# A macaron block on one core: V of the first half, the second half's tiles and the later tokens' transposes in the first half's slots

## What is computed

```python
x = x + 0.5 * ffn(layernorm(x))          # dense 512x512 + top-2 of 8 LoRA experts of rank 16
q = rope((n @ wq).reshape(B, S, 32, 128)); k = rope((n @ wk).reshape(B, S, 8, 128))   # n = layernorm(x)
v = (n @ wv).reshape(B, S, 8, 128)
scores = q . k * 128 ** -0.5, masked to j <= i and j > i - 128
x = x + (softmax(scores) @ v).reshape(B, S, 4096) @ wo
x = x + 0.5 * ffn(layernorm(x))
```

## Time and profile before

| | us |
|---|---|
| median of 3 runs (lowest, highest) | 746.47 (746.28, 747.5) |
| the profiled execution | 746.33 |
| its span in the trace | 744.6 |

### The profile page before, as it was taken

One profiled execution on the slowest core, in us unless ns is written; L12 is line 12 of the kernel. 1 busy time (PEld: TensorE's weight loads), 2 busy tenths in 40 slices (PEclk: granted clock), 3 DMA queues, 4 the chain that ended last, 5 costly groups with the idle time before them and its releaser, 6 DMA issues.

```text
span 744.6 us, 13949 instructions
## 1 busy us (share of the span) xinstructions
PE 717.2 (96%) x3692; PEld 603.1 (81%) x3692; DVE 601.0 (81%) x2060; ACT 413.3 (56%) x1122; POOL 396.5 (53%) x466
## 2 busy tenths in 40 slices
PE   8899789999999999999999999999999999998998
PEld 5787667888888888888888888888888888887786
DVE  6898778877887888878887888788878887788795
ACT  3324475657655676556655766576656665754320
POOL 0674268634864477438653765367535863462420
PEclk9999999999999999999999999999999999999999
DMA  8240003100220022002200120013000310030002
GB/s 266 73 158 16 0 3 98 43 1 2 73 70 1 0 70 70 0 0 70 56 14 0 56 70 14 0 32 94 15 0 0 99 28 1 1 114 1 0 31 85
DMA packets 25843, 32.13 MB, mean 43 GB/s; under 512 B 5833, under 2 KB 14281, under 8 KB 25298
## 3 DMA queue, kind: packets, MB, share of 16 engines
q1 hardware_dynamic: 25232, 30.69, 13.1%
q10 hardware_dynamic: 578, 1.05, 0.4%
HBM read 27.54 MB, written 4.19 MB: 43 GB/s over the span
## 4 chain that ended last, share of the span: by engine, by line
PE 70%; DVE 20%; issue 5%; ACT 3%; DMA 1%; POOL 1%; DVEq 0%; SPq 0%; ACTq 0%
PE bank L1102 26%; PE bank L1160 19%; PE bank L1145 6%; PE bank L1124 5%; PE bank L1068 5%; PE bank L1132 3%; DVE prob L822 2%; DVE rot L787 2%; DVE oT_lo L834 2%; DVE prob L814 1%; DVE sm L807 1%; PE bank L1121 1%; DVE rot L778 1%; ACT prob L550 1%; DVE pT_hi_lo L828 1%
## 5 line engine op out<-in xcount | busy, mean ns | idle before, releaser
L368 POOL TENSOR_TENSOR swap<-swap,rope 128x512 f32<-128x512 f32 x80 | 110.1, 1377 | 129.8 <-ACT swap L523 129.8
L550 ACT ACTIVATE prob<-sm,nmax 128x128 f32<-128x128 f32 x128 | 51.5, 403 | 151.4 <-DVE prob L814 150.4
L375 POOL TENSOR_SCALAR_AFFINE_SELECT pT_hi_lo<-pT_hi_lo 128x256 fp32r<-128x256 f32 x128 | 52.3, 409 | 140.3 <-DVE pT_hi_lo L828 139.8
L523 ACT ACTIVATE swap<-bank 64x512 f32<-64x512 f32 x160 | 94.9, 593 | 10.6 <-PE bank L1102 6.7
L558 ACT ACTIVATE pT_hi_lo<-bank 128x256 fp32r<-128x256 f32 x128 | 48.9, 382 | 71.5 <-PE bank L1132 50.6
L822 DVE TENSOR_SCALAR prob<-prob,rinv 128x128 f32<-128x128 f32 x256 | 83.3, 367 | 4.5
L385 POOL TENSOR_TENSOR q_lo<-rot,q_hi 128x512 fp32r<-128x512 f32 x64 | 82.6, 1291 | 6.9 <-ACT q_hi L531 6.9
L1160 PE MATMUL bank<-wo_hi,oT_hi 128*128 128x512 f32 x256 | 74.6, 413 | 5.0 <-DVE x L841 5.0
L828 DVE TENSOR_TENSOR pT_hi_lo<-bank,pT_hi_lo 128x256 fp32r<-128x256 f32 x128 | 53.6, 418 | 29.4 <-ACT pT_hi_lo L558 29.2
L1102 PE MATMUL bank<-xnT_hi,wq_hi 128*128 128x512 f32 x256 | 71.4, 391 | 2.2 <-DVE v_lo L798 1.4
L1102 PE MATMUL bank<-xnT_lo,wq_hi 128*128 128x512 f32 x256 | 73.4, 389 | 0.0
(11 more groups left out here) (150 smaller groups left out, 1768.9 us busy)
## 6 DMA issues: line engine op xcount, KB each, us to landing
raw<-in_L_attn_wq SPq DMA_DIRECT2D x32, 256.0 KB, 3.0
raw<-in_L_attn_wo SPq DMA_DIRECT2D x32, 256.0 KB, 2.6
x<-in_L_attn_x SPq DMA_DIRECT2D x4, 512.0 KB, 7.3
raw<-in_L_attn_wk SPq DMA_DIRECT2D x8, 256.0 KB, 2.7
raw<-in_L_attn_wv SPq DMA_DIRECT2D x8, 256.0 KB, 2.6
out<-x SPq DMA_DIRECT2D x8, 256.0 KB, 2.0
raw<-in_L_ffn_W_base ACTq DMA_DIRECT2D x4, 256.0 KB, 5.1
wb_keep_hi<-q_hi SPq DMA_DIRECT2D x1, 1024.0 KB, 4.9
```

The costliest lines, as they stand in the source:

```text
L368: nc.gpsimd.tensor_tensor(w, w, tab, ALU.mult).then_inc(t2_done, 1)
L523: last = nc.scalar.activation(swap[a:a + half, m % 2, :], A[m % 2][b:b + half, :], ACT.Copy)
L550: last = nc.scalar.activation(prob[:, s % 2, lo:hi], src, ACT.Exp, bias=nmax[:, s % 2, i:i + 1], scale=-1.0, accum_out=rsum[:, s % 2, i:i ...
```

## The change

The prologue projects only k and q of the first half (60 matmuls) and goes on to `scores(0)`. V of the first half (12 matmuls) and the transposes of tokens 6 and 7 go into slot 0 of group 0, and the six tiles of the second half follow in slots 1 to 7 in chunks of 12, 12, 12, 12, 12, 8 and 4 (`START`), not 9 in each of eight slots. `v_transpose(0)` and `v_hi`, `v_lo` go from slot 0 to slot 1, `v_transpose(0)` ahead of that slot's projection. The rstd of tokens 4 to 7 goes from VectorE to POOL, behind `rope_lo(0,0)`. The normalised tokens 6 and 7 are written in four half-width instructions into other places (one new tile, `spare`), and the transposes of tokens 4 to 7 go to banks 4 to 7. The SyncE queue is unchanged.

```diff
+START = (60, 72, 84, 96, 108, 120, 132, 140, 144)
+START_ENDS = {s: t for t in range(5, 12) for s in range(SLOTS) if START[s] < 12 * (t + 1) <= START[s + 1]}
...
+        spare = sb("spare", [P, 2 * P])
...
-            if ln == 1 and 4 <= t < 6:
-                return S[t % 2]
-            if ln == 1 and t >= 6 or ln == 2 and t >= 2:
+            if ln == 1 and t >= 4:
+                return bank[t]
+            if ln == 2 and t >= 2:
                 return bank[4 + t % 2]
...
+        def xn_half(ln, t, a):
+            if ln == 1 and t == 6:
+                return (sm, prob)[a][:, 1, 0:2 * P]
+            if ln == 1 and t == 7:
+                return ar_part[:, :, :].rearrange("p a n -> p (a n)")[:, 0:2 * P] if a else spare[:, :]
+            return xn_buf(ln, t)[:, a, :]
...
+        def tile_ends(g, hf, s, first, last):
+            if last and hf == 1:
+                return (0, None, 0), (0, None, 0)
+            if first and hf == 0:
+                split, end = START_ENDS.get(s - 1) if s > 1 else None, START_ENDS.get(s)
+                return tuple((t // 6, t % 6, t // 6) if t is not None else (0, None, 0) for t in (split, end))
+            return tuple((2 * g + hf + 1, ENDS.get(c), 1 - hf) for c in (s - 1, s))
... POOL, prologue
-            for m in range(6):
-                if m < 5:
-                    rope_sin(0, m)
-                if m:
-                    rope_lo(0, m - 1, 0)
+            pool.wait_ge(tables_landed, 32)
+            rope_sin(0, 0)
+            rope_sin(0, 1)
+            rope_lo(0, 0, 0)
+            norm_rstd(1, 4, NT)
+            rope_lo(0, 1, 0)
+            rope_sin(0, 2)
+            rope_sin(0, 3)
+            rope_lo(0, 2, 0)
+            rope_sin(0, 4)
+            rope_lo(0, 3, 0)
+            rope_lo(0, 4, 0)
... ScalarE, slots
+                        if start and s == 1:
+                            v_hi(0, 0)
                         softmax_exp(u, s)
-                        if s == 0:
+                        if start and s == 0:
+                            rope_hi(0, 2, 0)
+                            rope_swap(0, 4)
+                            x_hi(1, 6)
+                            x_hi(1, 7)
+                            rope_hi(0, 3, 0)
+                        elif s == 0:
                             v_hi(2 * g + hf, hf)
...
                         if m == 5:
-                            v_copy(2 * g + hf + 1)
+                            v_copy(jm)
+                            if start and s == 0:
+                                rope_hi(0, 4, 0)
... ScalarE, prologue: now swap(0,0), swap(0,1), hi(0,0), swap(0,2), hi(0,1), swap(0,3), x_hi(1,4), x_hi(1,5)
... VectorE, slots
-                        if s == 0 and not (last and hf == 1):
+                        if s == (1 if first and hf == 0 else 0) and not (last and hf == 1):
                             v_lo(2 * g + hf, hf)
...
                         softmax_norm(u, s)
                         if split is not None and split < 5:
-                            rope_sum(2 * g + hf + 1, split)
+                            rope_sum(js, split)
+                        if start and s == 0:
+                            rope_sum(0, 3)
+                            rope_cos(0, 4)
+                            x_lo(1, 6)
+                            x_lo(1, 7)
+                            rope_sum(0, 4)
... VectorE, prologue
             rope_cos(0, 0)
             norm_stats(1, NT - 2)
+            norm_stats(1, NT - 1)
             rope_sum(0, 0)
             rope_cos(0, 1)
-            norm_stats(1, NT - 1)
             rope_sum(0, 1)
             rope_cos(0, 2)
-            norm_rstd(1, 4, NT)
+            dve.wait_ge(rstd_done, 4)
             xn(1, 4)
             xn(1, 5)
+            rope_cos(0, 3)
+            softmax_min(0, 0)
             rope_sum(0, 2)
-            rope_cos(0, 3)
             xn(1, 6)
             xn(1, 7)
             x_lo(1, 4)
             x_lo(1, 5)
-            rope_sum(0, 3)
-            rope_cos(0, 4)
-            x_lo(1, 6)
-            x_lo(1, 7)
-            rope_sum(0, 4)
-            v_diff(0)
-            softmax_min(0, 0)
... TensorE, slots
-                        if s == 0 and not start:
+                        if s == (1 if first and hf == 0 else 0):
                             v_transpose(j)
-                        if start and s == 0:
-                            pe.wait_ge(xlo_done, 2 * NT)
-                        if not (last and hf == 1):
+                        if first and hf == 0:
+                            if s == 1:
+                                pe.wait_ge(xlo_done, 2 * NT)
+                            jp = START[s] // 72
+                            project(jp, jp, START[s] - 72 * jp, START[s + 1] - 72 * jp, 0)
+                            if s == 0:
+                                x_transpose(1, 6)
+                                x_transpose(1, 7)
+                        elif not (last and hf == 1):
                             project(j + 1, 1 - hf, FIRST[s], FIRST[s + 1], g + hf)
...
-                        if s == 0 and start:
-                            v_transpose(j)
... TensorE, prologue
             x_transpose(1, 4)
             x_transpose(1, 5)
-            project(0, 0, 60, 60 + 8, 0)
-            pe.wait_ge(x_out, 6)
-            x_transpose(1, 6)
-            x_transpose(1, 7)
-            project(0, 0, 60 + 8, 72, 0)
             scores(0, 0, 0, 0)
```

More of the change, by code:

```diff
@@ L401, in group @@
                     for s in range(SLOTS):
-                        split, m = (ENDS.get(c) if not (last and hf == 1) else None for c in (s - 1, s))
+                        (js, split, par), (jm, m, _) = tile_ends(g, hf, s, first, last)
                         if m is not None and m < 5:
-                            rope_sin(2 * g + hf + 1, m)
+                            rope_sin(jm, m)
                         if last and hf == 1 and s in (1, 5):
@@ L409, in group @@
                         if split is not None and split < 5:
-                            rope_lo(2 * g + hf + 1, split, 1 - hf)
+                            rope_lo(js, split, par)
                         weights(g, hf, s, last)
@@ L572, in group @@
                         start = first and hf == 0
+                        if start and s == 1:
+                            v_hi(0, 0)
                         softmax_exp(u, s)
-                        if s == 0:
+                        if start and s == 0:
[5 more added lines that the diff above has]
+                        elif s == 0:
                             v_hi(2 * g + hf, hf)
                         weights(g, hf, s, last, (0, 1))
-                        split, m = (ENDS.get(c) if not (last and hf == 1) else None for c in (s - 1, s))
+                        (js, split, par), (jm, m, _) = tile_ends(g, hf, s, first, last)
                         if m == 5:
-                            v_copy(2 * g + hf + 1)
+                            v_copy(jm)
+                            if start and s == 0:
+                                rope_hi(0, 4, 0)
                         elif m is not None:
-                            rope_swap(2 * g + hf + 1, m)
+                            rope_swap(jm, m)
                         if not (start and s == 0):
@@ L624, in _ @@
             act.wait_ge(kept, 32)
[L625 to L637, removed]
+            rope_swap(0, 0)
+            rope_swap(0, 1)
+            rope_hi(0, 0, 0)
+            rope_swap(0, 2)
+            rope_hi(0, 1, 0)
+            rope_swap(0, 3)
+            x_hi(1, 4)
+            x_hi(1, 5)
             group(0, True, False)
@@ L688, in xn @@
                 i = NT * ln + t
-                wait(dve, tr_done, i - 1)
-                nc.vector.tensor_scalar(xn_buf(ln, t), x[:, t, :].rearrange("p (a n) -> p a n", a=2), mv[:, t, 0:1], rstd[:, t:t + 1],
-                                        ALU.subtract, ALU.mult).then_inc(xn_done, 1)
+                if ln != 1 or t < 6:
+                    wait(dve, tr_done, i - 1)
+                if ln == 1 and t >= 6:
+                    for a in range(2):
+                        last = nc.vector.tensor_scalar(xn_half(ln, t, a), x[:, t, a * 2 * P:(a + 1) * 2 * P], mv[:, t, 0:1],
+                                                       rstd[:, t:t + 1], ALU.subtract, ALU.mult)
+                    last.then_inc(xn_done, 1)
+                else:
+                    nc.vector.tensor_scalar(xn_buf(ln, t), x[:, t, :].rearrange("p (a n) -> p a n", a=2), mv[:, t, 0:1],
+                                            rstd[:, t:t + 1], ALU.subtract, ALU.mult).then_inc(xn_done, 1)
             def x_lo(ln, t):
@@ L863, in group @@
                         start = first and b == 0
-                        split, m = (ENDS.get(c) if not (last and hf == 1) else None for c in (s - 1, s))
-                        if s == 0 and not (last and hf == 1):
+                        (js, split, _), (jm, m, _) = tile_ends(g, hf, s, first, last)
```

(3 more changed lines are left out.)

8 lines of the change are left out of this document (4 added, 4 removed).

## The result

The changed kernel takes 750.44 us (median of 5; 750.12 to 752.66), the kernel before 747.3 in the same comparison (746.28 to 747.61, 5 executions). The ratio is 1.0049, 95% interval [1.0033, 1.0065]: slower, by 0.5%. The profiled execution is the 750.44 one, its span 748.7 us, 4.1 more than before.

The account below looks back on a forecast made before the run. It took the loop VectorE, ScalarE, VectorE to bound the first eight slots and TensorE the rest from 123.4 us; 1.6 + 1.5 + 1.2 = +4.3 us on 746.33 gave 750.6, taken as 750.5, range 745.2 to 752.2.

Parts of the forecast that it names:

- One event decides: From 123.4 us on TensorE is the bound; moving the start of `v_transpose(1)`, 123.44 us, moves the end by as much.
- The removal from VectorE gains nothing: Prologue: with the rstd on POOL, `xn(1,4)` still ends at about 76.2 us, as before; `xn(1,5)` ends over 1 us later.
- Term one: Prologue to slot 1: `softmax_min(2)` starts at 96.2 instead of 94.66 us, +1.6 us; at full clock -0.1.
- the sign of being right: New profile: a TensorE stall of 3 to 4 us, ended by the subtraction of `v_diff`, with half clock behind it.
- half clock: TensorE at 1.2 instead of 2.4 GHz behind the stall at `v_transpose(0)`: 1.7 us lost in the 12 matmuls of k.
- Terms two and three: Slot 4 waits for the added swap and cos, +1.5 us; port waits on wo_lo in slots 5 and 6, +1.2 us.
- T: The start of `softmax_norm(4)`, at 105.73 us in the kernel before; times in slots 4 to 6 count from it.
- The sum: At `v_transpose(1)`: 1.6 + 1.5 + 1.2 = +4.3 us, giving 750.6, taken as 750.5 us.
- two cases of one kernel: Behind the stall at `v_transpose(0)`: half clock, 750.5 us, chance 42 in 100; or clock stays up, 749.0 us, 27.
- The faster rival: Prologue: VectorE, freed of 4.7 us of rstd, starts the loop 2.3 us earlier; about 744.3 us, chance 13 in 100.

Follow-up runs that it names:

- e9: The changed kernel with the rstd of tokens 4 to 7 back on VectorE and nothing in its place on POOL: 751.59 us, ratio 1.0065.
- e1: The changed kernel with 11 matmuls of no use put ahead of `v_transpose(0)`, into TensorE's stall in slot 1: 749.57 us, ratio 1.0041.
- e2: The changed kernel with `START` set so that the six second-half tiles end in the same slots as before the change: 748.22 us, ratio 1.0019.
- e5: The changed kernel with the edits of e2, e3 and e4 together: 745.02 us, ratio 0.9982.
- e10: e5 with matmuls of no use in two stalls, rstd on VectorE, and POOL's `rope_lo(0,1)` held until both `xn` are done: 743.58 us, ratio 0.9966.
- e3: The changed kernel with `v_transpose(0)` behind slot 1's 12 matmuls and `v_hi(0)` behind that slot's exponentials: 749.48 us, ratio 1.0040.
- e4: The changed kernel with POOL's `rope_lo(0,1)` waiting until the normalisation of tokens 4 and 5 is done: 750.64 us, ratio 1.0043.
- e8: The changed kernel with POOL's four wo_lo of slot 4 in group 0 waiting until `softmax_norm(5)` is done: 750.23 us, ratio 1.0043.

## Why the prediction was right, point by point

- **One event decides.** Right: `v_transpose(1)` 3.93 us later by distance (+4.3 said), rest of the span unchanged.
- **The removal from VectorE gains nothing.** Right: rstd ready at 74.55 (74.6 said), second `xn` done at 77.46 (77.9 said), and e9 shows it from the other side.
- **Term one, +1.6.** It was +1.11 (and 96.2 - 94.66 is 1.5, not 1.6). The stall ahead of `v_transpose(0)` is 2.85 us, not 3.6 (3 to 4 was named as the sign of being right), because `v_diff(0)` ends at 88.54 and not 89.0. Three errors are in that: the forecast had half clock from the first transposes on and `softmax_min(0)` at 79.9, but the clock stayed full until 78.4 and it started at 78.93; the last half-width `xn` then lost 1.05 us to the port (1.46 against 0.41), which the sum did not have; and `softmax_norm(0)`, with 0.48 us of scalings, lost none of the 0.8 us put there for `rope_sin(0,4)`. Behind it the half clock came as said and cost what was said: 4.87 - 3.24 = 1.63 us by e1, 1.7 forecast. At full clock the term was put at -0.1; e1, with a `v_transpose(0)` that starts 0.55 us later, measures +0.03.
- **Terms two and three, +2.7.** They were +2.84. `softmax_norm(5)` at T + 5.46 (T + 5.4 said), `x_add(0)` at T + 16.88 (T + 16.7 said); e2 takes both away.
- **The sum.** +4.3 was 0.4 too high: term one 0.5 too high, the other two 0.1 too low. 0.2 us came from elsewhere in the span: 746.33 + 3.93 + 0.2 = 750.4. That the forecast of 750.5 lies 0.1 us from the median is luck, for the changed kernel's own executions differ by 2.5 us, and the kernel before had 747.3 in this comparison and not the 746.47 from which the forecast started: the medians moved by 3.1 us, the forecast said 4.
- **What was not seen.** The forecast treated the half clock as a choice between two cases of one kernel. It is one of the execution: kernels with a stall of 2 to 3 us there have it in some executions and not in others, as far as the mean clocks tell. One stretch of 3.4 us at half lowers the mean over 745 us by 0.0023 (3.4 x 0.5 / 745). In 42 executions of the kernel before, from the comparisons of the experiments, the median is 746.4 us at a mean clock of 1.000 (13 of them), 746.8 at 0.998 (15) and 747.4 at 0.995 (12). So the "about 1.7 us of work lost" behind the first stall of the kernel before is not time lost at the end: there a step down in mean clock by one such stretch goes with 0.4 to 0.6 us. Behind `v_transpose(0)` of the changed kernel VectorE waits 3.10 us for `swap(1,0)`, which waits for the matmuls, and there e1 finds the whole 1.6 us. Why it costs less in the kernel before was not tested.
- **The faster rival** had its mechanism half right. With both `xn` free of the port and two more edits (e5, e10) `softmax_min(2)` starts 2.0 to 3.1 us earlier than before, and the time falls below the kernel before. But the `xn` are the smaller part of it: from e3 to e5, both at full clock up to there, they bring 0.64 us (30.12 to 29.48), and alone, in e4, nothing that the median shows. And it is not VectorE freed of the rstd that brings the gain: e10, with the rstd back on VectorE and POOL held back, is the earliest of all. The change lacked POOL held back, `v_transpose(0)` behind the matmuls and the old ends of the tiles; whether it needs all three was not run.

Open: how much of the gain in e3 is the order of the instructions and how much the clock; which stall of an execution with a low mean clock was followed by a drop, and what each such drop cost in the medians, since only one execution of each kernel has a profile.

## What to carry to other kernels

Work moved off a busy engine was no gain here, since the other engine shares a port with it (both `xn` are done at 77.46 us with the rstd on either): look at what will run beside it, and in which order they start. In a loop between two engines, count a slot by the engine that waits inside it (swap behind two weight copies), not by the one with room for a larger chunk. And find the one event that the rest of the span hangs on: its distance from a fixed start told edits of 1 us apart where medians of five could not, as long as the clock of the stretch is read beside it.

## What the runs showed of the hardware that was not expected

- VectorE's instructions of four elements a partition wait as long for the port as those of 512: 1.14 to 1.21 us instead of 0.16 (e9), about 1 us more, as for the `xn` of 512 (1.46 and 1.49 instead of 0.54).
- Stalls of 2.55 us (e3, ahead of slot 1's matmuls) and 2.67 us (e9, ahead of the transposes of token tile 4) were followed by full clock, stalls of 2.15 us (before) and 2.24 us (e8, for the last wo_lo) by half clock; one of 2.37 us lay in a stretch that was at half already (e4). The length of the stall alone does not say whether the clock falls.
